# Counting graph edges on TensorE: windows of five lanes of ten destinations, ten jobs innermost in the one-hot tiles

## What is computed

```python
def layer0(h, src, dst):                       # h = relu(layernorm(x))
    xn = batchnorm(h)
    agg = segment_sum(xn[src], dst, 1250) / max(deg, 1)
    conv = relu(agg @ W_conv + b_conv)
    attn = kernelized_attention(h[:256])       # 8 heads, 256 random features
    return batchnorm(conv + attn @ Wo + h)
x = x + layer0(h, src, dst)
h = relu(layernorm(x))
agg = segment_sum(h[src], dst, 1250)
z = relu(batchnorm(((1 + eps) * h + agg) @ W1 + b1))
x = x + h + relu(batchnorm(z @ W2 + b2))
```

## Time and profile before

| | us |
|---|---|
| median of 3 runs | 365.77 (365.72 to 365.85) |
| span of the profiled execution | 363.9 |
| PE busy, share of the span | 349.3 (96%) |
| DVE busy | 245.2 (67%) |
| ACT busy | 181.7 (50%) |
| POOL busy | 94.1 (26%) |

### The profile page before, as it was taken

One profiled execution on the slowest core, in us unless ns is written; L12 is line 12 of the kernel. 1 busy time (PEld: TensorE's weight loads), 2 busy tenths in 40 slices (PEclk: granted clock), 3 DMA queues, 4 the chain that ended last, 5 costly groups with the idle time before them and its releaser, 6 DMA issues.

```text
span 363.9 us, 6197 instructions
## 1 busy us (share of the span) xinstructions
PE 349.3 (96%) x2072; PEld 224.6 (62%) x2072; DVE 245.2 (67%) x666; ACT 181.7 (50%) x303; POOL 94.1 (26%) x163
## 2 busy tenths in 40 slices
PE   8999899989999999999998999999999999999994
PEld 4678655757777666767565675455555555565562
DVE  5889999998998995867996886522464453422325
ACT  0548538768477167454437766411533644233132
POOL 8132020000000000100042778722277465101100
PEclk9999999999999999999999999999999999999998
DMA  6990303300000000034900000000000000010223
GB/s 179 283 304 19 119 1 119 118 3 1 3 3 4 3 3 3 3 103 145 263 7 3 0 2 3 2 2 1 2 0 0 2 0 2 0 51 21 70 58 85
DMA packets 13539, 18.05 MB, mean 50 GB/s; under 512 B 1839, under 2 KB 6895, under 8 KB 13491
## 3 DMA queue, kind: packets, MB, share of 16 engines
q1 hardware_dynamic: 12538, 17.21, 16.3%
q10 hardware_dynamic: 953, 0.23, 0.3%
HBM read 14.88 MB, written 2.56 MB: 48 GB/s over the span
## 4 chain that ended last, share of the span: by engine, by line
PE 82%; DVE 6%; ACT 5%; issue 3%; POOL 2%; DMA 1%; DVEq 0%; SPq 0%; ACTq 0%; POOLq 0%
PE bank L1436 78%; PE bank L1466 2%; PE bank L1834 1%; POOL ln_s L491 1%; ACT hn L688 1%; PE bank L1793 1%; DVE st_row L1324 1%; ACT hh L832 1%; ACT sqr L694 1%; DMA edge<-src 1%; DVE x L1387 0%; PE bank L1647 0%; ACT hring L602 0%; DVE aggf L1344 0%; DVE hl L1305 0%
## 5 line engine op out<-in xcount | busy, mean ns | idle before, releaser
L1436 PE MATMUL bank<-AT,hh 125*128 125x400 f16 (+3 forms) x250 | 81.1, 332 | 1.0 <-DVE hl L1305 0.5
L1436 PE MATMUL bank<-AT,hl 125*128 125x400 f16 (+3 forms) x250 | 80.8, 331 | 0.0
L994 DVE TENSOR_SCALAR ring<-iota_code,code 125x250 f16<-125x250 f16 x200 | 46.1, 306 | 1.4 <-issue 1.4
L1436 PEld LDWEIGHTS bank<-AT,hh 125*128 125x128 f16 x250 | 24.1, 97 | 19.2 <-issue 1.1
L1436 PEld LDWEIGHTS bank<-AT,hl 125*128 125x128 f16 x250 | 24.2, 97 | 17.7 <-issue 0.2
L1436 PE MATMUL bank<-ring,S 125*128 125x250 f16 x200 | 33.5, 310 | 0.0
L1436 PE MATMUL bank<-a_hi,w_hi 128*128 128x400 f16 (+1 forms) x96 | 32.6, 339 | 0.0
L1436 PE MATMUL bank<-agg_hi,w_hi 128*128 128x400 f16 (+1 forms) x96 | 32.6, 339 | 0.0
L1436 PE MATMUL bank<-agg_hi,w_lo 128*128 128x400 f16 (+1 forms) x96 | 32.5, 338 | 0.0
L1436 PE MATMUL bank<-a_hi,w_lo 128*128 128x400 f16 (+1 forms) x96 | 32.5, 338 | 0.0
L1436 PE MATMUL bank<-agg_lo,w_hi 128*128 128x400 f16 (+1 forms) x96 | 32.5, 338 | 0.0
(11 more groups left out here) (236 smaller groups left out, 704.2 us busy)
## 6 DMA issues: line engine op xcount, KB each, us to landing
w_s<-w SPq DMA_DIRECT2D x4, 1024.0 KB, 5.0
x_in<-x SPq DMA_DIRECT2D x5, 448.0 KB
x<-x SPq DMA_DIRECT2D x2, 1120.0 KB
out<-x SPq DMA_DIRECT2D x6, 224.0 KB
wB<-wk SPq DMA_DIRECT2D x1, 1024.0 KB, 9.3
wA<-wq SPq DMA_DIRECT2D x1, 1024.0 KB, 14.3
wC<-w_conv SPq DMA_DIRECT2D x1, 1024.0 KB, 16.0
wB<-wv SPq DMA_DIRECT2D x1, 1024.0 KB, 6.0
```

Source lines behind the costliest of these rows:

```text
L994: return dve.tensor_scalar(ring[:, slot, j, a:b], iota_code[0:CH, a:b], code[:, bass.ds(c + j, 1)], float(-CODES * t), ALU.subtract, ALU.i ...
L1436: return pe.matmul(o, l, r, start=start, stop=stop, skip_group_check=True)
```

## The change

Edges are no longer laid out in chunks fixed in the list. The list lies as 125 rows of 160 edges, each row loaded with the edges that follow it up to 384 (`edge`, WIDE). Destinations are grouped in 125 lanes of ten (LANE); a lane gets the 256 edges (REACH granules of 32) that begin at the last granule that starts before it. PE picks them out with 20 matmuls against `first`, a 0/1 table from DVE (group "chosen"), so that two chunks of 128 edges a lane end up one edge a partition. A window of 50 destinations is five lanes, so it has ten jobs (JOBS): each a matmul of K = 128, 128 output rows and 100 columns (10 destinations x 10 source tiles, CPL), two of them adding into each of five strips of the bank.

`S` and `ring` have the ten jobs innermost, and each is made for a whole window by one `tensor_tensor` against `iota_jobs`. PE reads both with a step of 10 elements, 20 bytes. A window's bank is ordered by destination and then source tile; ACT's copy reads it with a step of 10 fp32. The exact path is taken by one flag (`irregular`), zero for these data; the pieces "codes", "ranges" and RG go. `edge` is loaded by two queues, SP's and ACT's, after DVE has filled its padding; ACT turns it to fp16. The idle matmuls are SPARE 14 and 10 instead of 20 and 5.

```diff
+GRAN = 32
+GPR = EROW // GRAN
+REACH = 8
+WIDE = (GPR - 1 + REACH) * GRAN
 W = 50
+LANE = 10
+LPW = W // LANE
+CPL = T * LANE
+CHUNKS = REACH * GRAN // P
+JOBS = LPW * CHUNKS
...
-SPARE = {"start": 20, "ranges": 5, "hT0": 3, "hT1": 3, "hT2": 4}
+SPARE = {"start": 14, "firsts": 10, "hT0": 3, "hT1": 3, "hT2": 4}
...
-        ring = place("ring", [CH, 2, G, CODES], F16, 112.75)
-        S = place("S", [CH, 2, P, G], F16, 128.5)
+        ring = place("ring", [P, 2, CPL, JOBS], F16, 112.75)
+        S = place("S", [P, 2, P, JOBS], F16, 116.75)
+        iota_jobs = place("iota_jobs", [P, P, JOBS], F16, 125.25)
...
         def counts_of(t):
-            return banks[COUNT_BANK[t]][0:L, 0:CODES].rearrange("p (h a b) -> p h a b", h=2, a=T)
+            return banks[COUNT_BANK[t]][0:L, 0:CODES].rearrange("p (d a) -> p a d", a=T)
...
         def _(sp):
-            for a, d in enumerate((dst_t, src_t)):
-                sp.dma_start(edge[:, a, 0, :], d[0:P, :]).then_inc(sem("d_edge"), 16)
-            sp.wait_ge(sem("s_epad"), 1)
-            for a, d in enumerate((dst_t, src_t)):
-                sp.dma_start(edge[0:NCH - P, a, 1, :], d[P:NCH, :]).then_inc(sem("d_edge"), 16)
+            sp.wait_ge(sem("s_pad"), 2)
+            for rows in EDGE_LOADS:
+                load_edges(sp, 0, *rows)
...
         def _(act):
 
+            act.wait_ge(sem("s_pad"), 2)
+            for rows in EDGE_LOADS:
+                load_edges(act, 1, *rows)
+            for a, name in enumerate(("d_dst", "d_src")):
+                act.wait_ge(sem(name), 16 * len(EDGE_LOADS))
+                act.activation(edge16[:, a, :], edge[:, a, :], ACT.Copy).then_inc(sem("s_edge16"), 1)
...
+            def one_hots(t):
+
+                if t >= 2:
+                    dve.wait_ge(sem("s_win"), t - 1)
+                jobs = slice(t * JOBS, (t + 1) * JOBS)
+                for o, n, values in ((S, P, lane1), (ring, CPL, code1)):
+                    ins = dve.tensor_tensor(o[:, t % 2], iota_jobs[:, 0:n, :],
+                                            values[:, jobs].unsqueeze(1).broadcast_to([P, n, JOBS]), ALU.is_equal)
+                ins.then_inc(sem("s_hot"), 1)
...
                 if t + 1 < NW:
-                    first_lanes(t + 1)
+                    one_hots(t + 1)
                 if t:
                     low_counts(t - 1)
-                further_chunks(t)
-                if t + 1 < NW:
-                    first_chunks(t + 1)
-                if t + 2 < NW:
-                    load_range(t + 2)
+                further_edges(t)
+                dve.reg_add(made, made, 1)
...
+            pe.wait_ge(sem("s_edge16"), 2)
+            pe.wait_ge(sem("s_first"), 1)
+            ps = open_group(pe, "chosen")
+            for a in (1, 0):
+                for c in range(CHUNKS):
+                    at = (a * CHUNKS + c) * LANES
+                    for g in range(GPR):
+                        e0 = g * GRAN + c * P
+                        ins = mm(ps[:, at:at + LANES], edge16[:, a, e0:e0 + P], first[:, g, 0:LANES], g == 0, g == GPR - 1)
...
-            def count(ps, t, j, a, b, start, stop):
-                return mm(ps[:, a:b], S[:, t % 2, :, j], ring[:, t % 2, j, a:b], start, stop)
+            def count(ps, t, j, start, stop):
+                k = j // CHUNKS
+                return mm(ps[:, k * CPL:(k + 1) * CPL], S[:, t % 2, :, j], ring[:, t % 2, :, j], start, stop)
...
-                for n, j in enumerate(CHUNK_ORDER[:-1]):
-                    if n % Q == 0:
-                        pe.wait_ge(sem("s_hot"), G // Q * t + n // Q + 1)
-                    count(ps, t, j, *CHUNK_COLS[j], n == 0, False)
+                pe.wait_ge(sem("s_hot"), t + 1)
+                for j in range(JOBS - 1):
+                    count(ps, t, j, j % CHUNKS == 0, j % CHUNKS == CHUNKS - 1)
```

More of the change, by code:

```diff
@@ L29 @@
 HB = HID // P
[L30 to L33, removed]
+EROW = E // L
+GRAN = 32
+GPR = EROW // GRAN
+REACH = 8
+WIDE = (GPR - 1 + REACH) * GRAN
 W = 50
 NW = N // W
[L36 to L46, removed]
+LANE = 10
+LANES = N // LANE
+LPW = W // LANE
+CPL = T * LANE
+CODES = LPW * CPL
+CHUNKS = REACH * GRAN // P
+JOBS = LPW * CHUNKS
+FAR = 2
+PAD_DST = 2000
 COLS = [(0, 450), (450, 400), (850, 400)]
@@ L123, in take @@
         used[bank] += 1
-    take("codes", 2)
-    take("ranges", 3)
+    take("chosen", 2)
+    take("firsts", 3)
     for slot in SLOTS:
@@ L385, in gnn_kernel, with load_edges @@
         out_t = out.rearrange("(t l) d -> l t d", l=L)
-        dst_t, src_t = (a.rearrange("(c e) -> c e", e=CH) for a in (dst, src))
+        def load_edges(eng, a, row0, rows, width):
+            e = (dst, src)[a]
+            eng.dma_start(edge[row0:row0 + rows, a, 0:width],
+                          bass.AP(e.tensor, e.offset + row0 * EROW, [[EROW, rows], [1, width]]))\
+               .then_inc(sem(("d_dst", "d_src")[a]), 16)
+        EDGE_LOADS = ((0, L - 2, WIDE), (L - 2, 1, 2 * EROW), (L - 1, 1, EROW))
         def w_t(w):
@@ L987, in lanes @@
[L987 to L997 removed]
+            ps = read_group(dve, "chosen")
@@ new lines, in _, with irregular_flag @@
+            own.step(dve.scalar_tensor_tensor(code_all[:], ps_dst, float(T), src_tile[:], ALU.mult, ALU.add))
+            dve.sem_inc(free[PLACE["chosen"][0]], 1)
+            own.step(dve.tensor_tensor(of_lanes(code1[:]), by_chunk(code_all[:]),
+                                       lane_code[:].unsqueeze(1).broadcast_to([P, CHUNKS, LANES]), ALU.subtract))
+            def irregular_flag():
+                ps = read_group(dve, "firsts")
+                own.mark(dve.memset(from_row[:, LANES:], float(EROW * L // GRAN - 1)))
+                own.mark(dve.tensor_copy(from_row[:, 0:LANES], ps[0:1, 0:LANES]))
+                own.step(dve.tensor_copy(n_falls[:], ps[0:1, P:P + 1]))
+                dve.sem_inc(free[PLACE["firsts"][0]], 1)
+                own.step(dve.tensor_tensor(span_row[:], from_row[:, 1:], from_row[:, 0:LANES], ALU.subtract))
+                own.step(dve.tensor_reduce(longest[:, 0:1], span_row[:], AX.X, ALU.max))
+                own.step(dve.tensor_scalar(longest[:, 1:2], longest[:, 0:1], float(REACH - 1), None, ALU.is_gt))
+                own.step(dve.tensor_tensor(irregular[:], longest[:, 1:2], n_falls[:], ALU.add))
+                dve.sem_inc(sem("s_flag"), 1)
@@ L1160, in further_chunks @@
[L1160 to L1173 removed]
+            far = Own(dve, sem("own_far"))
```

279 lines of the change are left out of this document (105 added, 174 removed), and 4 rows, old and new, of tables (LONE_BANKS, SLOTS).

## The result

The changed kernel takes 388.96 us (median of 4 runs, 386.39 to 391.23) against 365.76 (365.72 to 365.85) for the kernel before in the same runs: a ratio of 1.0633, interval 1.0588 to 1.0679. It is 23 us slower; the forecast was 352.0, 14 us faster. The time lies outside the range of 348 to 380.

What follows compares the result with a forecast made beforehand. PE's own matmuls were taken to bound the stretch from 20 to 160 us, DVE close behind. Terms -13.0 -2.6 +1.0 +1.0 +0 -0.2 = -13.8 us took 365.77 to 352.0; range 348 to 380, the forecast's own 348 to 356.

Steps and rivals of the forecast that it cites:

- The step that failed: In PE's windows: a moving column at 20 bytes costs 0.48 ns, 48 ns for 100, hidden behind the load.
- second rival: PE's windows: moving reads stretched four times, 1.8 us a window, +15.8 us in 25, 379 us in all; chance 0.28.
- 25 windows on PE: Ten short matmuls a window take 0.65 us instead of 1.17, saving 13.0 us in 25 windows.
- DVE's three waits: PE's waits before QT0, G3 and KV1, laid to DVE, end as DVE's window work shrinks: -2.6 us.
- hT4 and hT9: PE's two waits for ACT: the savings of windows 0 and 2 are lost again there, +1.0 us.
- ACT, banks: New waits on ACT, whose copy reads PSUM at 40 bytes, +1.0 us (0 to 4); later bank release taken as 0.
- head: Start of the kernel up to the first K piece: taken as 0, between -0.3 and +1.5 us.
- RG: Its four records between K0 and K1 go: -0.2 us.
- First rival, half rate: PE's windows: moving columns at half rate, 0.088 us a job, 0.88 a window; 357 to 362 us, chance 0.22.
- Third, DVE at one element a cycle: DVE's new instructions take twice 1.65 us a window, 366 to 375 us; chance 0.08 together with new ACT and bank waits.
- The rule of lines: Skill's rule that two accesses should hit each 16-byte line, so PE's 20-byte moving reads slow by an amount not given.

Runs made afterwards that it cites:

- e_pairs: e_ring_pairs with S also stored in pairs of jobs (step of 4 bytes) and one short iota serving both tiles; 356.38 us, ratio 0.976 to the kernel before.
- e_steps: Separate kernel of nothing but matmuls, stepping the moving and the stationary operand from 2 to 64 bytes; 100 moving columns take 44 ns at 2 bytes, 179 at 20.
- e_edges: Changed kernel with each edge load of 123 rows cut into 112 and 11 rows; 385.84 us, ratio 1.057 to the kernel before.
- e_flat: Changed kernel with ring stored job after job, so PE reads it contiguously and DVE writes it with a step; 424.9 us, ratio 1.164 to the kernel before.
- e_scalars: Changed kernel with ring stored job after job and made by ten tensor_scalars with contiguous output; 365.95 us, ratio 1.0016 to the kernel before.
- e_keys: Changed kernel with e_edges' loads, GpSimd waiting for keys before iota_jobs, iota_code and ATlo's clear after the third row scale; 383.75 us, ratio 1.049 to the kernel before.
- e_ring_pairs: Changed kernel with ring stored in pairs of jobs: PE reads at a step of 4 bytes, DVE writes contiguously; 359.52 us, ratio 0.981 to the kernel before.
- e_best: e_pairs with e_edges' loads, ATlo's clear and the search for falls moved later, idle matmuls dealt 19 and 4; 352.47 us, ratio 0.965 to the kernel before.

## Why the prediction was wrong, and where it was right

**The step that failed** is the price of a moving column at 20 bytes: "By that a moving column at 20 bytes costs 0.48 ns as well, 48 ns for 100, and stays hidden behind the load." Measured: 1.8 ns, 179 ns for 100. It had two links. S's load at 16 bytes was taken for an ordinary load with 13% on top, because 145 ns is near the 137 of 125 columns. It was a quick one, stretched: at a step of 4 bytes it takes 98 ns (e_pairs) and paces at 25 ns or less, at 16 bytes it paces at 59 (e_steps). And its price for a column, 59/128 = 0.46 ns and so indeed near the 0.48, was carried from loads to moving columns. A load goes over lines four times as fast as a moving operand does. The factor would have carried over (for loads 59 against at most 25, for moving columns 4.0), as the second rival had it; the absolute price did not. The earlier trace rows fitted both readings, as the prediction says, and the choice between them decided 27 us. I had put 0.42 on one and 0.28 on the other where the rows gave no ground for a preference.

| term of the sum | predicted | measured |
|---|---|---|
| 25 windows on PE | -13.0 (0.65 us each) | +16.5 (1.83 us each) |
| DVE's three waits | -2.6 | gone; all waits together -3.6 |
| hT4 and hT9 | +1.0 | inside the -3.6: longer windows fill them |
| ACT, banks | +1.0 | 0: AT's copy 589 ns, 607 before |
| head | 0 (-0.3 to +1.5) | +7.3 |
| RG | -0.2 | -0.2 |
| clock | not in the sum | about +3, what is left over |

**The second rival** gave the windows +15.8 and 379 us. Its mechanism and its size for the windows were right (0.18 us a job, e_steps 0.181). What it lacked were the head (7.3) and the clock (about 3), and small sums on the windows (+0.7) and waits (-1.0); so its time was 10 us short too, and the range that ended at it did not hold 389. The numbering is not the same throughout the prediction: the two rivals that its part on the window calls second and third stand first and second in its list.

**The head.** The prediction counted POOL's elements at 1.92/1024 us each and looked for a delay of the first ln_s behind POOL. The elements cost more, iota_jobs 4.17 us for 1280, but that was not the point. The chain ran over the loads: "how much slack the first K piece has for that no row here shows", it said, and gave it at most 1.5 us. The added wait was DVE's, for all destinations, and behind it on DVE stood the row statistics that the first hring needs; the prediction's order of work on DVE should have had that. In the kernel before DVE waited for edges too, but they came at 3.97 in loads of 128 and 32 rows. Taken apart, the 7.3 us are: +6.5 for the landing (10.49 against 3.97), of which the number of rows, 123, makes 5.6 (e_edges: 4.92); +0.7 for DVE's work from there to the row statistics, in which the cast beside a busy GpSimd has 1.7; -1.3 for the table load, which did move ahead as predicted; and +1.4 for the ten idle matmuls in front of PE's transposes, which the prediction had "before that".

**First rival, half rate**: wrong; the doubling comes at 8 bytes (90 ns), at 20 it is fourfold. (The upper case of its sum gives 362.6, not 362.) **Third, DVE at one element a cycle**: wrong in the changed kernel, DVE's 821 and 672 ns are a little under S's old rate (predicted 0.93 and 0.72), and the three waits went. But with a stepped output DVE did become the bound (e_flat), and with ten short instructions its waits came back (e_scalars); so the innermost jobs do for DVE what they were priced at.

**The rule of lines.** The prediction weighed a rule of the Trainium skill ("SBUF — State Buffer", section "Door 1: The DMA port swizzle"), two hits to a line of 16 bytes, against S's row and took the row. The rule's direction was right; the step that it calls free, 8 elements or 16 bytes, was not: e_steps shows the cost starting above 4 bytes and complete at 16.

## What to carry to other kernels

Before an operand is laid out for the engine that writes it, price how TensorE reads it: for a moving fp16 operand the step of 20 bytes cost four times the contiguous time, and the same tile in pairs (step of 4 bytes) cost nothing on either side. A stall that is hidden in the trace (S's load, 145 ns beside 97) tells of a mechanism whose price on the critical operand has to be bounded by its factor and not only by its nanoseconds. And of a new wait in the head, follow both what has to land (with its number of rows) and what runs beside the first instruction that it releases.

## What the runs showed of the hardware that I had not expected

- Moving fp16 columns at a step of s bytes take 0.11 ns x s each between 4 and 16 bytes, 0.44 below and 1.7 to 1.8 above; loads of 128 columns rise in the same way from 8 bytes on, at about a quarter of the time a column (e_steps).
- The granted clock falls to 1.2 GHz for 3.4 or 6.8 us at a time among the windows. In the changed kernel, e_edges and e_keys (0.95 to 0.96 from 20 to 160 us) and in e_steps PE had been busy for 5 us and more before each fall, with moving columns at 16 bytes or more among its reads. That these reads bring it down is what those runs suggest, not what they show, and they are not the only occasion: in e_scalars (contiguous) it falls twice as PE comes out of a wait of 2.1 and 2.2 us, in e_ring_pairs and e_best (4 bytes) once, 2.3 and 1.3 us after a wait of 1.0 and 2.2. e_pairs has no fall among its windows.
- A window that reads at 20 bytes is not slower in such a fall: in e_keys the one at 47.29, with 1.0 us of it in the fall, takes 1.94 us, as the same window of the changed kernel does at the full clock. At 4 bytes two windows within the fall of e_best take 0.81 and 0.92 us, and in e_pairs 0.47 and 0.55.
- A DVE tensor_tensor with an output step of 200 bytes takes 4.78 ns an element, with a contiguous one 0.67 (e_flat); with two or ten innermost elements it is the same 0.67.
- A cast of 6 elements waits out a 4 us instruction of GpSimd that only writes (3.59 us instead of 0.17).
- iota on GpSimd costs by more than its elements: 1280 in 128 rows of ten 4.17 us, 1024 in 128 rows of eight 1.92, 256 in 128 rows of two 1.52, 500 in one row 0.55.
- ACT's copy out of PSUM with a step of 40 bytes takes 589 ns where it took 607 from runs of 25 adjacent columns.
